# Places of their own for the first two batches and the setup, in a one-core kernel of two attention layers, a diffusion step and a time-gated norm block

## What is computed

```
x = L0(x, t):   h = two small layers on a noise encoding of t; scale, shift = h @ Wsc, h @ Wsh
                out = silu(scale * LN(x) + shift) @ W_in + b_in        LN over the whole 256 x 256
                out = silu(scale * LN(out) + shift) @ W_out + b_out;   return out + x
x = L1(x, mask, timestep, bias):
                x = LN(x) * (1 + scale) + shift;  q, k, v = x @ Wq, x @ Wk, x @ Wv    (16 heads of 16)
                scores = q k^T / 4 + bias, masked with -inf;  x = x + softmax(scores) v @ Wo
                x = x + gelu2(LN(x) @ W1) @ W2
x = L2(x, dt):  x = max(x + dt * (differences of A*x and B*x along both axes), 0)
x = L3(x, gate): causal attention of 16 heads on LN(x), then gelu(LN(x1) @ W1) @ W2; x + gate * (x2 - x)
```

## Time and profile before

| | us |
|---|---|
| median of 3 runs | 2784.4 |
| lowest, highest | 2781.39, 2788.78 |
| the profiled execution | 2785.6 |
| its span, first to last instruction | 2784.3 |
| TensorE busy | 2617.9 (94%) |
| ScalarE busy | 2344.9 (84%) |
| VectorE busy | 2239.9 (80%) |
| GpSimd busy | 1698.3 (61%) |

### The profile page before, as it was taken

How to read it: one execution, slowest core, us unless ns; L and a number is a source line. 1 busy time by engine, 2 the same in 40 slices (tenths; PEclk the granted TensorE clock), 3 DMA queues, 4 the chain that set the end, 5 groups by cost and what they waited for, 6 DMA issues and landing times.

```text
span 2784.3 us, 62626 instructions
## 1 busy us (share of the span) xinstructions
PE 2617.9 (94%) x20072; PEld 2222.1 (80%) x20072; DVE 2239.9 (80%) x7925; ACT 2344.9 (84%) x5285; POOL 1698.3 (61%) x1742
## 2 busy tenths in 40 slices
PE   7778999999999999999999999999999999999998
PEld 6656888888888888888888888788888888888776
DVE  6567888888888888888888888888888888888763
ACT  2456899988998998889899888889988889998875
POOL 3456666566666666666665666666566766666431
PEclk9888999999999999999999999999999999999998
DMA  6223333333333333334333333333333333333211
GB/s 231 87 91 108 111 114 99 101 105 100 105 116 113 100 103 105 99 105 117 112 100 103 109 94 105 114 113 97 101 108 98 105 115 115 95 105 103 77 28 31
DMA packets 176405, 287.96 MB, mean 103 GB/s; under 512 B 45840, under 2 KB 99088, under 8 KB 175696
## 3 DMA queue, kind: packets, MB, share of 16 engines
q1 hardware_dynamic: 176080, 283.97, 34.6%
HBM read 174.64 MB, written 8.45 MB: 66 GB/s over the span
## 4 chain that ended last, share of the span: by engine, by line
PE 70%; ACT 8%; SPq 5%; issue 3%; DMA 2%; DVE 2%; POOL 0%; ACTq 0%; DVEq 0%; POOLq 0%
PE bank L1148 15%; PE bank L1141 14%; PE bank L1169 11%; PE bank L1126 10%; PE bank L1118 7%; PE bank L1161 5%; SPq L382 4%; PE bank L1133 3%; DMA Ks<-KU 2%; ACT PB L960 2%; PE bank L1187 2%; ACT BB L981 2%; PE bank L1276 2%; SPq L378 2%; PE bank L1188 2%
## 5 line engine op out<-in xcount | busy, mean ns | idle before, releaser
L960 ACT ACTIVATE PB<-PB,mx 128x256 f32<-128x256 f32 (+1 forms) x2048 | 841.5, 475 | 11.4 <-DVE mx L756 10.5
L764 DVE TENSOR_TENSOR PO<-bank,PH 128x384 f16<-128x384 f32 (+1 forms) x1024 | 589.7, 617 | 151.8 <-ACT PH L966 147.8
L467 POOL TENSOR_TENSOR BT<-BT,MN 128x1024 f32<-128x1024 f32 x256 | 547.4, 2138 | 124.9 <-DMA BT<-in_bias 124.1
L1161 PE MATMUL bank<-Ks,Qs 96*128 96x512 f32 (+1 forms) x1024 | 525.6, 516 | 79.7 <-DVE mx L756 40.6
L966 ACT ACTIVATE PH<-bank 128x384 f16<-128x384 f32 (+1 forms) x1024 | 503.4, 540 | 109.9 <-PE bank L1169 108.2
L1169 PE MATMUL bank<-ident,PB 128*128 128x128 f32 x3584 | 495.0, 277 | 17.4 <-DVE PO L764 12.9
L756 DVE CUSTOM_DVE_ANT_0 PB<-bank,BT 128x256 f32<-128x256 f32 x1024 | 390.0, 418 | 118.3 <-issue 86.8
L1169 PEld LDWEIGHTS bank<-ident,PB 128*128 128x128 f32 x3584 | 420.5, 143 | 62.5 <-ACT PB L960 28.8
L756 DVE CUSTOM_DVE_ANT_0 PB<-bank,caus 128x128 f32<-128x128 f32 (+1 forms) x1024 | 322.1, 352 | 55.7 <-PE bank L1161 35.0
L1187 PEld LDWEIGHTS bank<-VP,PH 128*128 128x128 f16 x3584 | 205.1, 96 | 120.7 <-issue 108.3
L1161 PEld LDWEIGHTS bank<-Ks,Qs 96*128 96x128 f32 x1024 | 195.9, 192 | 110.5 <-DMA Ks<-KU 47.5
(11 more groups left out here) (225 smaller groups left out, 5248.6 us busy)
## 6 DMA issues: line engine op xcount, KB each, us to landing
BT<-in_bias SPq DMA_DIRECT2D x256, 512.0 KB, 3.9
Qs<-QH SPq DMA_DIRECT2D x512, 64.0 KB, 2.5
Ks<-KH SPq DMA_DIRECT2D x1024, 32.0 KB, 2.0
Qs<-QU SPq DMA_DIRECT2D x256, 64.0 KB, 2.7
Ks<-KU SPq DMA_DIRECT2D x512, 32.0 KB, 2.0
XT<-in_xT SPq DMA_DIRECT2D x32, 256.0 KB, 4.5
X<-in_x SPq DMA_DIRECT2D x32, 256.0 KB, 2.9
AB<-ada_rows SPq DMA_DIRECT2D x32, 256.0 KB, 3.3
```

The lines of the kernel that those rows point to most:

```text
L467: G.op.tensor_tensor(v2(BT[k % 3]), v2(BT[k % 3]), MN[:, :].unsqueeze(1).broadcast_to([128, 2, 512]), ALU.add).then_inc(g_bt, 1)
L764: V.op.tensor_tensor(PO[i][:, 0:w], bP[h][:, 0:w], PH[i][:, 0:w], ALU.subtract).then_inc(v_low, 1)
L960: S.op.activation(o, o, ACT.Exp, scale=-1.0, bias=mx[u.layer][:, c:c + 1]).then_inc(a_exp, 1)
L1161: T.op.matmul(bS[q][:, 0:2 * w].rearrange("p (h k) -> p h k", h=2), Qs[i][0:96, et * 256 + q * 128:et * 256 + q * 128 + 128], k2[:, :, 0:w ...
```

## The change

`OWN` gets an entry for batch 0 and one for batch 1, with places for nearly all their pieces (those absent keep the place of `P`), and the pieces of the setup get other places in `P`. No function is touched, and no instruction is added or taken away. The line numbers of the changed kernel are 33 higher from `place` on.

```
@@ P @@
-    "ld_w1": -11, "ld_sten": -21, "ld_w3": -100, "coefs": -12,
+    "ld_w1": -28, "ld_sten": -41, "ld_w3": -191, "coefs": -20,
-    "film_a": -71, "film": -65, "adas": -46, "scr": -41,
+    "film_a": -91, "film": -65, "adas": -59, "scr": -58,
@@ OWN @@
+    0: {
+        "score0_1": -6, "score1_1": -3, "bias0_1": -3, "bias1_1": -3, "exp0_1": 0, "exp1_1": 0, "flip0_1": 1,
...
+    },
+    1: {
+        "score0_1": 0, "score0_3": 0, "score1_1": 1, "bias0_1": 2, "bias0_3": 3, "exp0_1": 4, "exp0_3": 4,
...
+    },
```

More of the change, by code:

```diff
@@ L111 @@
         "st_out": 1129,
+    },
[11 rows of a table added]
+        "w1_gelu": 68, "w2": 70, "f1": 77, "s_pm": 82, "s_b": 93, "s_r": 83, "s_rp": 94, "s_re": 97, "s_ha": 96,
+        "s_w": 98, "s_ab": 98, "s_row": 98, "s_mm": 102, "s_f": 102, "m3": -55, "m3_rstd": -54, "m3_norm": -52,
[3 rows of a table added]
+    },
[4 rows of a table added]
+        "stack_3": -4, "ld_x": -116, "ld_xn": -91, "ld_ab": -33, "ld_mask": -68, "mask": -37, "n1_ones": -70,
[6 rows of a table added]
+        "w1_out": 62, "w1_gelu": 68, "w2": 69, "f1": 75, "s_pm": 75, "s_r": 78, "s_rp": 79, "s_ha": 98, "s_w": 98,
[3 rows of a table added]
     },
```

## The result

The changed kernel took 2761.45 us (median of 4 runs, 2758.68 to 2763.53), the kernel before beside it 2782.89 us (4 runs, 2781.39 to 2788.78). The ratio is 0.9918, with a 95% interval of 0.9900 to 0.9936: 21.4 us faster, where the forecast was 14.4 us under the 2784.4 known then. A second set of 6 runs of the same code gave 2762.17 us and a ratio of 0.9918 (0.9904 to 0.9933). The direction and the place of the gain are as predicted, the range (2760 to 2781) holds the time, and the size was forecast too small. The profiled execution took 2763.53 us; its lines have numbers 33 higher than those of before.

What follows compares the result with a forecast made beforehand. TensorE bounds from about 290 us; before it, a chain of latencies. The ramp's gain, between 13.2 and 18.7, was taken as 15.0, less 0.6 setup: 14.4 us. From 2785.6 that gives 2771.2, less 1.2: 2770.0 us, range 2760 to 2781.

Steps and rivals of the forecast that it cites:

- The setup: VectorE in the setup: n1_sum.b0 ahead of film_a.b0 makes film_a and all of batch 0 0.6 us later.
- Units, start: Batch 0's unit 0: its flips go ahead of unit 2's score, at about 70.3 instead of 74.65, 4.3 us sooner.
- Units, pitch: Batch 0's units: a loop of 3.9 us each, a GpSimd-bound step at u6, u7's flips at 105.3.
- Batch 1's first part: W_out.b1 at 98.8 among batch 0's units, c1 and t1 back to back, k1_lo.b1 near 121: 11.0 us sooner.
- Batch 1's units: Batch 1's first scores at 128.5, 11.5 us sooner; x1.b2 at 171.0 instead of 186.77, 15.8 us sooner.
- Batch 2: Some 1.3 us given back at t1.b2; scores of b2's u0 behind q3 at 202.0 instead of 215.22, 13.2 us.
- rival 2: More than forecast: later half-clock products (q1.b2, c1, t1, o1, s_mm.b1) run full and short waits stay away; 22 us, 2762.4, 12%.
- Layer 3 and b3: Unit 1's flips of b2 at 217 instead of 234.21, 17 us; s_mm.b1 behind W_out.b3 adds up to 1.7 us.
- short waits: Waits between engines, 0.03 to 0.1 us each, some twenty per stage, left out by the walk; about 3 us taken off.
- my last sentence: A gain given back in the steady part was held impossible while TensorE is busy for 97% of it.
- Rival 1: Half is lost inside batch 0's units: ScalarE's high0.u7 waits behind x1_norm.b1; gain 5.0 us, 2779.4 us, 20%.
- Rival 3: Slower: batch 0's unit loop stays at half clock, 6.6 us a unit; 10 us lost, 2795.0 us, 8%.

Runs made afterwards that it cites:

- score_first: The changed kernel with unit 2's first score ahead of unit 0's flips again on TensorE, flips of later units moved back likewise; 2779.61 us, ratio 0.9987.
- front1: The changed kernel with batch 1's own places only up to its layer-1 units, the later ones at the common places; 2772.82 us, ratio 0.9946.
- before_sten: The kernel before with only the nine later stencil places of batch 1 (s_pm to s_f) added; 2783.00 us, ratio 0.9999.
- own0: The changed kernel without batch 1's own places, batch 0's kept; 2794.93 us, ratio 1.0037.
- after_again: The changed kernel once more, same code, 6 runs; 2762.17 us, ratio 0.9918.
- exp_early: The changed kernel with exp0 of a batch 0 unit ahead of the previous unit's high copies again on ScalarE; 2766.10 us, ratio 0.9917.
- best: The code of exp_early run once more against the changed kernel, 6 runs; 2759.36 us, ratio 0.9914.
- before_warm: The kernel before with 24 unread TensorE products behind W_out and 24 ahead of t1, for batches 1 and 2; 2786.23 us, ratio 1.0010.
- after: The changed kernel itself in its first set of 4 runs, against the kernel before; 2761.45 us, ratio 0.9918.

## Why the prediction was right, and where it was too small

1. **The setup, 0.6 us later.** Right at film_a (17.75 against 17.15); behind it within the scatter.
2. **Units, start.** u0's flips: forecast 70.3, measured 71.53 (3.1 us sooner than before, not 4.3; the 1.2 between them are the later first score). The cause is shown by score_first: with the old order the wait of 3.7 us comes back.
3. **Units, pitch.** Forecast for u1 to u7: 77, 82.5, 88, 92, 96, 101.4, 105.3; measured 77.03, 80.90, 86.39, 90.33, 94.14, 99.65, 103.46. The loop of 3.9 us is right (3.94 and 3.81 for u3 to u5), and so is the step at u6 (5.5 against 5.4; mask_add.u6 ends at 96.37, forecast 98.0). The step from u1 to u2 is 1.6 us shorter than mine, because I had the clock rise one unit later: the flips of u1 already take 0.66 us. That u1 itself agrees to 0.03 us is luck: its start is 1.2 us late, and the step to it is 1.2 us short, since there too the clock had risen.
4. **Batch 1's first part.** Forecast 98.8 for W_out, 110.4 and on for c1 and t1, 121 for k1_lo; measured 97.06, 108.28, 119.14. All are 1.7 to 2.1 us sooner, which is step 3's error carried on. q1 ran at full clock, as forecast (1.89).
5. **Batch 1's units.** x1.b2: forecast 171.0, measured 167.81. 2.1 us of the difference were there at b1's scores already (128.5 against 126.40), 1.1 are new, and no run separates them.
6. **Batch 2: the step that failed.** I took 31.0 us from x1.b2 to b2's first score (202.0 - 171.0); it took 26.5 (194.34 - 167.81), where before took 28.5. (My terms, 1.3 and 1.9 us given back, make 12.6 out of 15.8 and not the 13.2 that I wrote; so 0.6 of the error is in my sum.) The 1.3 us at t1.b2 did not come: from x1.b2 to t1.b2 it is 7.2 us in both kernels. From t1.b2 to v1.b2 it is 9.2 us against 10.0: q1.b2 ran at full clock, 1.89 us from 178.53 against 3.78, but o1 ahead of it took 2.75 us instead of 2.01. q1.b2 at full clock was a term of rival 2, to which I gave 12%. From v1.b2 to the score it is 10.1 us against 11.2. The product q3.b0 that stands in there (190.75) takes up a part of the wait between two w1 products, which start 3.56 us apart with it and 2.92 without: 0.6 us and not 1.9. And t2.b1 now stands ahead of v1.b2, so the first w1 product follows v1 after 1.83 us instead of 3.69. That term I had put at nothing without a reason. For q1, q3 and t2 this is read from the two traces; no run moved them alone.
7. **Layer 3 and b3.** Forecast 17 at unit 1's flips of b2 and up to 1.7 more behind; measured 25.3 there, 26.7 at the first score of layer 3, 26.3 at b3. The two steps are right in size: from b2's scores to unit 1's flips 3.8 forecast and 4.4 measured, behind it 1.0 at b3. But front1 shows that this needs the later places of batch 1, above all the stencil's, which carry 10.7 us at layer 3; I had counted them with 1.7 us at s_mm alone. before_sten shows that the stencil's don't do so by themselves.
8. **The sum and the rest.** At b3 the gain is 26.3 against the 14.4 of my sum. Of these 12 us, 8.3 stand at unit 1's flips of b2 already, 3.7 are what I took off for short waits, and 0.6 the setup; 0.7 go against it (1.0 of the 1.7 came). At the end 21.4 are left by the medians, against my last sentence, though no run shows that the order costs time there. That the stretch from 1000 to 1400 lies at 388 us of 400 (387.87) was right and proved nothing of the parts without such a stretch. So the forecast is 7 us too small, what is left of an error of 12 us in the ramp and one of 5 against it. That the time lies in the range, 1.5 us above its lower end, is luck to this extent: with 26.3 us at the end it would be below 2760.

Rival 1 (half is lost inside the units) did not come: among ScalarE's waits from 92 to 110 us there is none for x1_norm.b1's input. Rival 3 did not come in the changed kernel. But own0 is the slower case, by another mechanism than mine, the chain falling behind the units, and with the size that I had given to rival 3 (10 us). Rival 2 names the right cause for a part of what I missed, the clock, and has nearly the time (2762.4). In the first profile only q1.b2 came of its terms, while W_out.b2 and c1, t1 and o1 of that stage still ran at half clock or below full; in after_again c1, t1 (0.66 us each) and o1 (1.89) are at full clock too, and b2's scores come at 192.10. So 12% was too little for it.

## What to carry over

Sets of places that lose or give nothing alone (batch 0's, +9.8 us; the 23 of batch 1's chain, 0) can be parts of a change that gains 21 us, so an order is to be judged as a whole: walk every engine in its new order and ask at each step of a chain which ready work stands behind it. The same holds for taking one order back: the old places of the flips cost most of the gain among the new places around them, though the kernel before ran well with them. A wait removed in a ramp can give back more than itself, since the products behind it no longer run at half clock; here that was 6 to 7 of 26 us. And before a gain in front is followed to the end of the span, compare two profiles of the same code: in the steady part here they differ by as much as 9 us, with the number of short stretches at half clock.

## What the runs showed that I had not expected

- The same instructions have two tempos in the steady part, 80.6 and 81.0 to 82.1 us for a batch, both at full clock, the second with some 1 us more of wait for the stacking transfers at the first score of unit 6. Busy TensorE in 400 us is 387.9 to 388.0 in the one and 384.1 to 384.5 in the other. In 12 of 14 profiles the switch comes at batch 17, whatever the time.
- Short stretches at half clock appear in the steady part although TensorE is busy for 97% of it: none in exp_early, 20.5 us in all in best, which is the same code, and 9.3 us lie between the two from b3 to b31.
- A wait of 2.33 us on TensorE was followed by a product at 3.62 us instead of 1.99; in before_warm 48 passes in place of the idle time kept the next product at 1.99.
- With nearly one order of instructions ahead of it, the first score of the program moves by about 2 us from profile to profile (66.58 to 68.38 before, 67.83 to 69.93 after the change). b1's scores, 58 us behind it, are the same to 0.02 us in after and after_again, whose first scores stand 0.4 us apart, but 1.7 us apart in exp_early and best, whose first scores stand 1.8 apart.
